# Moving steps in a rotary attention loop, and half of a top-eight search ahead of the activations

## The reference, cut to what matters

```python
# rotary attention, 16 heads of 8 channels
q, k = rms_norm(rotate(q)), rms_norm(rotate(k))
att = softmax(causal(q @ k.T / sqrt(8)))          # per sequence and head, 256 x 256
x = x + (att @ v).reshape(B, T, C) @ W_proj.T
# product keys, 8 heads
s1, i1 = top_k(sim1, 8); s2, i2 = top_k(sim2, 8)  # each of 32 similarities
fs, pk = top_k(s1[..., :, None] + s2[..., None, :], 8)   # best 8 of the 64 sums
hidden = gelu(xn @ expert_down[fi]) * relu(fs)
x = x + hidden @ expert_up[fi]
```

## Time and profile before

| what | us |
|---|---|
| median of 3 runs (2662.86 to 2665.55) | 2663.31 |
| the profiled execution's own time | 2666.33 |
| its span, first to last instruction | 2664.6 |
| rotary loop, first shift to last statistics | about 1328 to 1589 |
| first product keys, tiles | about 1612 to 2062 |
| second product keys, tiles | about 2206 to 2663 |
| busy over the span: PE, DVE, ACT, POOL | 2092.7, 2249.4, 1863.0, 1620.6 |

### The profile page before, as it was taken

How to read it: one execution, slowest core, us unless ns; L and a number is a source line. 1 busy time by engine, 2 the same in 40 slices (tenths; PEclk the granted TensorE clock), 3 DMA queues, 4 the chain that set the end, 5 groups by cost and what they waited for, 6 DMA issues and landing times. The chain is left out here.

```text
span 2664.6 us, 59310 instructions
## 1 busy us (share of the span) xinstructions
PE 2092.7 (79%) x17450; PEld 1738.0 (65%) x17451; DVE 2249.4 (84%) x5529; ACT 1863.0 (70%) x4276; POOL 1620.6 (61%) x1481
## 2 busy tenths in 40 slices
PE   6558888879599999693588877888888448888888
PEld 3246666757588888473466656777777237777777
DVE  7589999865688888657888857999999788999998
ACT  4689999656555555563255548999998349999997
POOL 0079999637200000375566538999999209999997
PEclk9779999989899999797699988999999769999999
DMA  2023333151200000111100000000000000000000
GB/s 49 2 68 95 97 95 100 56 152 51 58 1 0 0 0 1 53 52 38 41 2 0 0 1 1 0 0 0 0 0 0 1 0 1 8 4 4 4 4 8
DMA packets 67622, 69.82 MB, mean 26 GB/s; under 512 B 10248, under 2 KB 46304, under 8 KB 67488
## 3 DMA queue, kind: packets, MB, share of 16 engines
q1 hardware_dynamic: 59408, 56.33, 7.1%
q0 software_dynamic: 4992, 10.23, 1.4%
q10 hardware_dynamic: 3088, 1.62, 0.2%
HBM read 56.50 MB, written 11.67 MB: 26 GB/s over the span
## 5 line engine op out<-in xcount | busy, mean ns | idle before, releaser
L1973 POOL TENSOR_TENSOR k5a_psums<-k5a_sims 128x1024 f32<-128x1024 f32 x224 | 421.6, 1913 | 17.3 <-DVE k5a_w L2181 12.0
L1973 POOL TENSOR_TENSOR k7a_psums<-k7a_sims 128x1024 f32<-128x1024 f32 x224 | 421.7, 1914 | 13.9 <-DVE k7a_w L2181 8.7
L1068 POOL TENSOR_TENSOR mc_hc<-mc_h,mc_cs 128x512 f32<-128x512 f32 x256 | 327.8, 1296 | 32.9 <-DVE mc_h L1035 17.5
L2038 PE MATMUL k5a_pw<-g_ident,k5a_w 128*128 128x128 f32 x2048 | 265.5, 277 | 70.6 <-DVE k5a_hid L2189 45.9
L2038 PE MATMUL k7a_pw<-g_ident,k7a_w 128*128 128x128 f32 x2048 | 262.0, 276 | 70.1 <-DVE k7a_hid L2189 45.9
L2038 PEld LDWEIGHTS k5a_pw<-g_ident,k5a_w 128*128 128x128 f32 x2048 | 226.7, 141 | 113.9 <-DVE k5a_w L2181 52.9
L1035 DVE TENSOR_TENSOR_SCAN mc_h<-mc_dA,mc_inj 128x512 f32<-128x512 f32 x256 | 298.8, 1200 | 2.4 <-PE mc_inj L924 1.8
L2038 PEld LDWEIGHTS k7a_pw<-g_ident,k7a_w 128*128 128x128 f32 x2048 | 227.3, 141 | 109.4 <-issue 63.8
L2181 DVE SCALAR_TENSOR_TENSOR k7a_w<-k7a_psums,k7a_best,k7a_lift 128x1024 f32<-128x1024 f32 x224 | 279.6, 1272 | 0.5 <-ACT k7a_lift L2109 0.3
L2181 DVE SCALAR_TENSOR_TENSOR k5a_w<-k5a_psums,k5a_best,k5a_lift 128x1024 f32<-128x1024 f32 x224 | 279.1, 1270 | 0.5 <-ACT k5a_lift L2109 0.3
L2109 ACT ACTIVATE k7a_lift<-k7a_psums 128x1024 f32<-128x1024 f32 x224 | 229.2, 1023 | 37.6 <-DVE k7a_w L2181 33.2
(11 more groups left out here) (503 smaller groups left out, 5863.2 us busy)
## 6 DMA issues: line engine op xcount, KB each, us to landing
mc_cs<-c_rows SPq DMA_DIRECT2D x128, 256.0 KB, 3.1
e_w<-in_L_ffn_W_dram SPq DMA_DIRECT2D x16, 256.0 KB, 5.5
token_rows<-e_zn SPq DMA_DIRECT2D x16, 256.0 KB, 3.7
e_zn<-token_out SPq DMA_DIRECT2D x16, 256.0 KB, 5.1
out_dram<-g_X SPq DMA_DIRECT2D x7, 256.0 KB, 2.3
e_zs<-token_rows,e_token POOLq DMA_INDIRECT x78, 2.6
token_out<-e_ys,e_token POOLq DMA_INDIRECT x78, 2.3
g_X<-in_L_attn_a_x_dram SPq DMA_DIRECT2D x4, 256.0 KB, 4.7
```

The lines of the kernel that those rows point to most:

```text
L1068: nc.gpsimd.tensor_tensor(hc[:, q % RH, :], h_[:, q % RB, :], cs[:, S % RC, :], ALU.mult).then_inc(outs, 1)
L1973: nc.gpsimd.tensor_tensor(psums[:, h - 1, :, :], rows_of(p, h), s2, ALU.add).then_inc(pooled, 1)
L2038: ins = nc.tensor.matmul(pw[:, j, :], w[:, h % WR, j * P:(j + 1) * P], env.ident[:, :], start=(h == 0 and j % 4 == 0), stop=(h == HD - 1 a ...
```

## The change

In the product keys `top8` gets a parameter `half`. The first half (heads 0 to 3, with the waits) goes ahead of `finish`, the second stays where the whole stood. In the rotary loop, on TensorE: `shift` goes ahead of mix 2 in step 0; `project` goes from step 7 to step 2 of the next round; `turn_back` from step 3 to 4; `place_y` from step 5 to 6, behind mix 1. On VectorE: `residual` goes from step 7 to step 3 of the next round (now of `seq(-2)`), `normalise` from step 4 to 5. On ScalarE: `enter_y` from step 6 to 7. The steps after the last round grow from eight to twelve.

```diff
-                def top8(t, p):
-                    need(dve, crossed, t)
-                    hold(dve, s_in, t + 1)
-                    for h in range(HD):
+                def top8(t, p, half):
+                    if half == 0:
+                        need(dve, crossed, t)
+                        hold(dve, s_in, t + 1)
+                    for h in range(half * HD // 2, (half + 1) * HD // 2):
                         for s in range(2):
                             ins = nc.vector.max(top[:, h, s, :], sims[:, p, h, s, :])
-                    ins.then_inc(topped, 1)
+                    if half:
+                        ins.then_inc(topped, 1)
...
                         weigh(t, p, 0)
+                        if not final:
+                            top8(t + 1, 1 - p, 0)
                         if not begun:
                             finish(t - 1, 1 - p)
                         weigh(t, p, 1)
                         if not final:
-                            top8(t + 1, 1 - p)
+                            top8(t + 1, 1 - p, 1)
...
+            PROJECT, RESIDUAL = 2, 3
...
-                run(NB // 2 - 1, NB == 2, True, range(2 * STEPS, 3 * STEPS))
+                run(NB // 2 - 1, NB == 2, True, range(2 * STEPS, 3 * STEPS + RESIDUAL + 1))
...  ScalarE
-                    if w == 6 and seq(-1):
+                    if w == 7 and seq(-1):
                         enter_y(*seq(-1))
...  TensorE
                 def step(w, seq):
+                    if seq(0):
+                        shift(*seq(0), w)
                     if w == 0 and seq(-1):
                         mix(*seq(-1), 2)
-                    if seq(0):
-                        shift(*seq(0), w)
                     if w < 6 and seq(1):
                         score(*seq(1), w)
                     if w == 1 and seq(-1):
                         mix(*seq(-1), 3)
-                    if w == 3 and seq(-1):
+                    if w == PROJECT and seq(-2):
+                        project(*seq(-2))
+                    if w == 4 and seq(-1):
                         turn_back(*seq(-1))
-                    if w == 5 and seq(-1):
-                        place_y(*seq(-1))
                     if w == 5 and seq(0):
                         mix(*seq(0), 0)
-                    if w == 6 and seq(0):
-                        mix(*seq(0), 1)
-                    if w == 6 and seq(1):
-                        turn_max(*seq(1))
-                    if w == 7:
-                        if seq(2):
-                            for g in range(4):
-                                place(*seq(2), g)
+                    if w == 6:
+                        if seq(0):
+                            mix(*seq(0), 1)
                         if seq(-1):
-                            project(*seq(-1))
+                            place_y(*seq(-1))
+                        if seq(1):
+                            turn_max(*seq(1))
+                    if w == 7 and seq(2):
+                        for g in range(4):
+                            place(*seq(2), g)
...  VectorE
-                    if w == 4 and seq(-1):
+                    if w == RESIDUAL and seq(-2):
+                        residual(*seq(-2))
+                    if w == 5 and seq(-1):
                         normalise(*seq(-1))
...
-                    if w == 7:
-                        if seq(2):
-                            for g in range(4):
-                                enter(*seq(2), g)
-                        if seq(-1):
-                            residual(*seq(-1))
+                    if w == 7 and seq(2):
+                        for g in range(4):
+                            enter(*seq(2), g)
```

More of the change, by code:

```diff
@@ L2201, in _ @@
                 dve.wait_ge(floored, 1)
-                top8(0, 0)
+                top8(0, 0, 0)
+                top8(0, 0, 1)
                 form(0, 0)
```

## The result

The changed kernel takes 2670.65 us (median; 2666.86 to 2677.25), the kernel before, timed beside it, 2667.03 (2662.86 to 2671.25): ratio 1.0015, 95% interval 1.0008 to 1.0022. It is a little slower, inside the 0.2% that I had called no change, where I had forecast 2650. The profiled execution has a span (first to last instruction) of 2667.7 against 2664.6.

A forecast was written before the change was run, and what follows sets the result against it. VectorE was taken to hold both product-key stages, and no single engine the rotary loop. Product keys -19.6 and rotary +6.1 took the profiled 2666.3 to 2652.8, or 2649.8 against the median, forecast as 2650; range 2637 to 2661.

The forecast's parts named there:

- Part 1: Product keys: half the search ahead of `finish` covers its wait for TensorE; tiles of 14.22 and 13.76, -19.6 us.
- stood 0.69 before the third ones: Product keys: TensorE's stand before a tile's third sums, taken to cover first sums that start 0.23 later.
- Part 2: Rotary loop: the moved residual costs VectorE more than its old slot gives back; round 16.6 against 16.07, +6.1 us in all.
- 11.98 + 1.2 - 0.1: Rotary loop, VectorE from first maximum to next first copy: old length, plus residual, less a wait of the shift; 13.1.
- come 1.2 later: Rotary loop: casts of Q behind the moved residual start 1.2 later, but their reader is four steps on.
- C: Rival, rotary loop: TensorE's stand at `turn_back` isn't covered, +1.1 a round, 13 in all, 2663; chance 0.06.
- D: Rival, rotary loop: the 1.1 us stand throws TensorE to 1.2 GHz, +9.8 a round, 2689 with four; chance 0.04.
- A: Rival: rotary gains too, as the residual finds cover; round 15.4, total -28, 2635; chance 0.13.
- E: Rival, product keys: the split does nothing, `finish` being late for its three waits, not TensorE; 2669; chance 0.04.
- B: Rival, product keys: half the gain, -12, as `finish` waits again in the second stage; 2657; chance 0.18.
- The tail: End of the rotary loop: last `turn_back` waits for projection and residual, +1.3, with some 0.6 given back; +0.7.
- 0.6 counted for round 1: Rotary loop: round 1 loses its residual, 15.5 against 16.07, a saving of 0.6.

The follow-up runs named there:

- filler: pk_only with the next tile's first hidden products put ahead of TensorE's first sums in the product keys; 2644.84 us, ratio 0.9915 to the kernel before.
- early_free: Changed kernel with the residual's signal to TensorE given after the addition instead of after the statistics; 2672.54 us, ratio 1.0024 to the kernel before.
- res_12: Changed kernel with projection and residual one step earlier, in steps 1 and 2 instead of 2 and 3; 2668.07 us, ratio 1.0004 to the kernel before.
- cast_first: Changed kernel with VectorE's casts of Q ahead of the residual in step 3; 2668.44 us, ratio 1.0003 to the kernel before.
- pk_only: Kernel before with only the split of the top-eight search, rotary loop unchanged; 2653.41 us, ratio 0.9949 to the kernel before.
- three_quarter: The split search alone, with 12 instead of 8 of the 16 MAX8 ahead of `finish`; 2658.27 us, ratio 0.9962 to the kernel before.
- no_gp: Changed kernel with GpSimd's selections and subtractions of the rotary loop cut to a few columns; 2658.86 us, ratio 0.9968 to the kernel before.
- q_first: Changed kernel with GpSimd's subtraction of Q, which waits for the casts, ahead of that of K; 2666.74 us, ratio 1.0005 to the kernel before.

## Why the prediction was wrong

**Part 1, a term that was put at nothing.** The mechanism and the tile were right: no new wait before `finish`, 14.21 and 13.77. Its full gain is what filler shows. From the first to the last weighing of head 0 the two stages take 886.3 in the kernel before (1620.71 to 2065.68 and 2204.53 to 2645.90) and 865.8 in filler (1620.74 to 2060.32 and 2198.18 to 2624.42): 20.5 against the 19.6 of the forecast. Another 1.0 of filler's 21.5 of span lies between the two stages; its cause is open. In the changed kernel 14.5 arrive. I had weighed the clock for the rotary loop alone. For the product keys I wrote that TensorE "stood 0.69 before the third ones", and used that stand as a cover; I didn't add up what would become of it: the 1.49 for `finish` and the delay of 0.57 in one piece in the first stage (2.05), 1.49 and 0.23 in the second (1.71). Six tiles at 0.80 and one at 1.26 make 6.1. (The Trainium skill, page "TensorE: Matmul & The Clock Gate", section "HAM oscillation — how this bites in real kernels", says that pauses between groups of matmuls can throw the clock back; the trace agrees, with 0.50 granted after a stand of 2.05 and 1.00 in all settled tiles once the stand was split, but only in about every fifth tile.)

**Part 2, the step that failed.** "Now it is 11.98 + 1.2 - 0.1 ..., or 13.1": it is 13.73. The residual's 1.2 was right (1.26), the slot that it left too (3.59 for 3.5). Of the casts I wrote that they "come 1.2 later", and looked only for who reads them; that they could get longer I put at nothing. They came into GpSimd's way and took 0.66 more (1.11 for 0.45). With the smaller differences the round is 17.32 for 16.6: 12 rounds x 0.72 = 8.6. (The Trainium skill, page "SBUF — State Buffer", section "Who interferes with whom", says that VectorE's casts and copies in some modes and its operations with two SBUF inputs share a port with GpSimd, and that its reductions don't; the trace agrees: the casts stretch, and the maxima beside GpSimd's work keep 0.6 each, though these read PSUM.)

**Rivals.** C fell: the stand at `turn_back` is 1.16, as forecast, and covered (early_free, res_12); with the residual 0.5 later it starts to show (cast_first). D came in small: its clock was down for a part of the round only, and two rounds at 0.91 cost 2.5, where D had 9.8 a round; the same effect came more often in the product keys, where I hadn't put it. A fell with the rounds of 17.32, E with the gain of pk_only. In the product keys the gain is 14.5, between B's 12 and the forecast's 19.6, but not by B's mechanism, as `finish` doesn't wait. The tail cost 0.1 instead of 0.7.

**The account by spans.** From the forecast's -13.5 to +3.1 are 16.6. The rotary loop has 10.7 of them (16.8 for 6.1): 8.6 for the twelve settled rounds, 2.5 more for the two long ones, 0.4 because the first rounds saved 0.2 and not the 0.6 counted for round 1 (from first maximum to first copy it took 12.32, 1345.35 to 1357.67, and not 11.98), less 0.6 for the tail; as rounded, these make 10.9. The product keys have 5.1: 6.1 of clock, less the 0.9 by which the tiles' gain was larger. The 0.7 ahead of the rotary loop lies within what runs differ by: with the same instructions ahead of it the first maximum starts at 1311.49 in pk_only, 1312.44 in the kernel before, and 1315.47 in three_quarter.

What stays open: why the clock falls in about one tile in five and in two rounds in twelve, when their neighbours have stands of the same length.

## What to carry to other kernels

An instruction that moves takes its neighbours along: look at what each other engine does at the moment to which it moves, above all GpSimd beside VectorE's casts and small SBUF operations. When a wait is taken away from one engine, add up the stands of the others again; two short stands of TensorE that become one can cost its clock, and independent work put into that stand gave back a third of the gain here (7.5 of 21.5). A residual or a statistic does best in a wait that the loop has anyway (rounds of 15.70 here), not where its input happens to be ready (17.32).

## What the runs showed of the hardware

A cast of 128x256 from float32 to bfloat16 takes 0.28 alone (no_gp, and the second cast of q_first), 0.51 beside GpSimd's selection and 0.75 beside its subtraction (changed kernel), and the other side pays as well: GpSimd's four copies of values, which lie beside the casts in the kernel before, take 0.90 there, and 0.76 in the changed kernel, where none runs beside them. GpSimd's timeline, kernel before:

```profile
1463.41 0.90 POOL L2606 COPY r_held<-r_V 128x64 f32 x4
```

TensorE's clock fell although the engine was busy 12.14 of 14.22 us of that tile, after one stand of 2.05; and the cost of 0.80 came one tile later and on another engine. In the settled tiles of a stage it fell once after stands of 1.71 (changed kernel, second stage), twice after stands of 1.88 (three_quarter, second), six times after 2.05 (changed kernel, first) and seven times after 2.33 (three_quarter, first), and never where a tile has two stands, of 1.49 and 0.69 (kernel before) or of 1.16 and 0.84 (filler, first stage).
